# Batch 1's transposes, first projections and values placed between the first row maxima of an attention and mixture-of-experts kernel

## What is computed

```python
x = L0_attn_x                                   # (4, 512, 256)
mod = (_silu(L0_c) @ L0_wmod).reshape(L0_c.shape[0], 6, 1, -1)
sa, ca, ga, sb, cb, gb = (mod[:, 0], mod[:, 1], mod[:, 2], mod[:, 3], mod[:, 4], mod[:, 5])
ga = (2 * (ga >= 0) - 1) * jnp.maximum(jnp.abs(ga), 0.25)      # gb in the same way
h = _layernorm(x, axis=-1) * (1 + ca) + sa
x = x + ga * _L0_attn_ref(h, wq, wk, wv, wo)    # 16 heads of 16, scores without a scale, softmax
h = _layernorm(x, axis=-1) * (1 + cb) + sb
x = x + gb * _L0_ffn_ref(h, ...)                # shared expert and the top 4 of 32 experts
```

## Time and profile before

| | us |
|---|---|
| median of 3 runs (604.32 to 607.96) | 604.84 |
| the profiled execution, as a run | 604.01 |
| its span, first to last instruction | 602.2 |
| TensorE busy | 563.6 (94%) |
| VectorE busy | 370.8 (62%) |
| ScalarE busy | 255.3 (42%) |
| mean granted TensorE clock | 0.974 |

### The profile page before, as it was taken

The page is one execution under the profiler, slowest core; times in us unless marked ns, Lnnn a source line. Parts: engine busy times, 40 slices in busy tenths (PEclk is TensorE's granted clock), DMA queues, the critical chain, the costliest instruction groups (busy, mean ns, idle before and its releaser), DMA issues.

```text
span 602.2 us, 10736 instructions
## 1 busy us (share of the span) xinstructions
PE 563.6 (94%) x3118; PEld 313.8 (52%) x3119; DVE 370.8 (62%) x860; ACT 255.3 (42%) x519; POOL 217.8 (36%) x284
## 2 busy tenths in 40 slices
PE   4889999999999999999999999998999999999881
PEld 3443233333333333333343465668888898897570
DVE  6385677778589785898855569435444444443683
ACT  3113545564765647555568140022343443433000
POOL 6100000000110751108434653441675666667332
PEclk9966999999999999999999999999999999999996
DMA  7242126100501224012101169524555645540791
GB/s 227 42 132 97 34 54 188 37 11 10 115 4 34 93 70 115 7 31 90 53 1 41 66 267 330 147 82 130 158 157 151 182 144 165 166 124 9 269 371 58
DMA packets 42343, 67.18 MB, mean 112 GB/s; under 512 B 9291, under 2 KB 32212, under 8 KB 41948
## 3 DMA queue, kind: packets, MB, share of 16 engines
q1 hardware_dynamic: 30208, 45.62, 25.9%
q0 software_dynamic: 7680, 16.87, 8.2%
q10 hardware_dynamic: 4416, 4.20, 2.1%
HBM read 38.93 MB, written 27.51 MB: 110 GB/s over the span
## 4 chain that ended last, share of the span: by engine, by line
PE 81%; DVE 8%; issue 3%; DMA 3%; SPq 1%; ACT 1%; POOL 1%; ACTq 0%; POOLq 0%; DVEq 0%
PE ps L863 23%; PE ps L876 10%; PE ps L1089 9%; PE ps L1110 6%; PE ps L960 6%; PE ps L812 5%; PE ps L954 3%; PE ps L834 3%; PE ps L1075 3%; PE ps L821 3%; PE ps L889 3%; DVE max_q L1201 2%; PE ps L1100 2%; PE ps L798 2%; PE ps L919 1%
## 5 line engine op out<-in xcount | busy, mean ns | idle before, releaser
L1201 DVE TENSOR_REDUCE max_q<-ps 128x1 f32<-128x512 f32 x256 | 163.8, 686 | 74.5 <-PE ps L834 72.8
L691 ACT ACTIVATE probs<-ps 128x512 f32<-128x512 f32 x256 | 138.0, 596 | 99.5 <-PE ps L863 99.2
L834 PE MATMUL ps<-k_rows,q_rows 31*128 31x512 f32 x512 | 149.7, 678 | 1.8 <-DMA k_rows<-qk_raw 1.8
L863 PE MATMUL ps<-q_rows,k_rows 32*128 32x512 f32 x512 | 147.6, 646 | 0.9 <-DVE max_q L1201 0.9
L545 POOL DMA_INDIRECT results<-y_sb,dest x96 | 94.5, 984 | 64.8 <-issue 35.0
L863 PEld LDWEIGHTS ps<-q_rows,k_rows 32*128 32x128 f32 x512 | 42.9, 186 | 71.6 <-ACT probs L691 52.2
L1089 PE MATMUL ps<-up_sb,oT 128*128 x384 | 70.7, 328 | 1.5 <-DVE oT L1565 1.3
L876 PE MATMUL ps<-probs,v_ext 128*32 128x512 f32 x512 | 68.2, 605 | 1.1 <-ACT probs L691 1.1
L1089 PEld LDWEIGHTS ps<-up_sb,oT 128*128 128x128 f32 x384 | 61.4, 191 | 2.1 <-issue 1.9
L1110 PE MATMUL ps<-down_sb,e_hidT 96*128 x192 | 49.8, 383 | 3.8 <-ACT e_hidT L748 3.8
L498 POOL TENSOR_TENSOR rstd<-veps,mhalf 128x4 f32<-128x4 f32 x4 | 4.1, 1036 | 134.3 <-DVE veps L1283 132.4
(11 more groups left out here) (180 smaller groups left out, 695.7 us busy)
## 6 DMA issues: line engine op xcount, KB each, us to landing
xe<-dispatched SPq DMA_DIRECT2D x96, 129.0 KB, 2.1
up_sb<-results SPq DMA_DIRECT2D x16, 512.0 KB, 7.9
up_sb<-in_up SPq DMA_DIRECT2D x2, 3072.0 KB, 15.1
dispatched<-pad_rows SPq DMA_DIRECT2D x33, 129.0 KB, 4.5
down_sb<-in_down SPq DMA_DIRECT2D x1, 3072.0 KB, 31.3
x<-in_x ACTq DMA_DIRECT2D x4, 512.0 KB, 5.1
q_rows<-qk_raw SPq DMA_DIRECT2D x64, 32.0 KB, 1.9
k_rows<-qk_raw SPq DMA_DIRECT2D x64, 32.0 KB, 1.9
```

The costliest lines, as they stand in the source:

```text
L691: act.activation(probs[:, u % 8, :], ps[:, st_bank(t.b, g, u), :], ACT.Exp).then_inc(exp_done, 1)
L834: pe.matmul(ps[:, banks[u % len(banks)], :], q_rows[32 * i:32 * i + ONE, b % 2, g, qt * P:(qt + 1) * P], k_rows[32 * i:32 * i + ONE, b % 2 ...
L863: pe.matmul(ps[:, st_bank(b, g, n), :], k_rows[32 * i:32 * i + 32, b % 2, g, kt * P:(kt + 1) * P], q_rows[32 * i:32 * i + 32, b % 2, g, :] ...
L1201: dve.tensor_reduce(max_q[:, g % 2, qt, i:i + 1], ps[:, banks[(16 * g + n) % len(banks)], :], AXX, ALU.max).then_inc(max_done, 1)
```

## The change

In the lead, batch 1's TP0, TP1, QK0, QK1 and V0 are computed between the 16 scores of group 0 and behind them. Only six scores of group 1 are made before turn 0 (22 in all, `AHEAD_BY`), and the turn begins when 16 maxima are done. Places 0 to 4 (`CATCH`) of turn 0 then issue four scores each, 22 to 41; from place 5 on it is two, the same ones as before. `FIRST` no longer has TP0, TP1, QK0, QK1 and V0; MAX0 goes from place 0 to 5, V1 from (27, 29) to 7, QK2 from (19, 21) to 13, QK3 from 23 to 19; V1 and QK2 are no longer split. ACT's work follows: it normalises batch 1 before the lead's values, and the new work goes ahead of and behind the negation of the first maxima. VectorE finishes batch 1's statistics ahead of its first maximum. On SP the first maxima go ahead of the fourth group's rows, batch 1's q rows ahead of MAX0, its k rows ahead of MAX1, and the shared expert's weights behind the two broadcasts. `raw_qk` waits for the rows of two groups instead of four. `scoreT` number 2 waits for batch 1's V0, the new last use of bank 7.

```diff
@@ -55,10 +55,12 @@
-    LEAD = ("TP0", "TP1", "QK0", "QK1", "QK2", "QK3", "V0", "V1", "MAX3")
-
-    FIRST = {"MAX0": 0, "TP0": 1, "TP1": 3, "QK0": 5, "QK1": 7, "MAX1": 8, "MOD0": 9, "MOD1": 11, "V0": (13, 15),
-             "MAX2": 16, "MODT": 17, "QK2": (19, 21), "QK3": 23, "MAX3": 24, "V1": (27, 29), "NT0": 30, "NT1": 31}
+    LEAD = ("TP0", "TP1", "QK0", "QK1", "QK2", "QK3", "V0", "V1")
+
+    AHEAD = {"TP0": 0, "TP1": 1, "QK0": 0, "LEAD_MAX": 1, "QK1": 0, "V0": 1}
+
+    FIRST = {"MAX0": 5, "V1": 7, "MAX1": 8, "MOD0": 9, "MOD1": 11, "QK2": 13, "MAX2": 16, "MODT": 17, "QK3": 19,
+             "MAX3": 24, "NT0": 30, "NT1": 31}
@@ -80,6 +82,9 @@
         elif self.att:
+            if self.mod:
+                for name, m in self.AHEAD.items():
+                    self.take(name, m, used)
             half = 0
@@ -286,12 +291,15 @@
         fin = Finish(B, used)
+        lead.uses["MAX3"] = turns[0].uses.pop("LEAD_MAX")
         turn_of = dict(zip(range(-1, B + 1), [lead, *turns, fin]))
...
         ONE = P // G - 1
+        AHEAD_BY = 22
+        CATCH = 5
@@ -323,6 +331,17 @@
             return h2T[:, s, k, :] if s < B - 1 else h2T_late[:, k, :]
+
+        def scores_at(t, place):
+
+
+            if t.mod and place < CATCH:
+                ahead = range(AHEAD_BY + 4 * place, AHEAD_BY + 4 * place + 4)
+            elif place < 16 or t.pre:
+                ahead = (32 + 2 * place, 33 + 2 * place)
+            else:
+                ahead = ()
+            return [(t.b + u // 64, u // 16 % NG, u % 16) for u in ahead]
@@ -380,16 +399,21 @@
+                if t.mod:
+                    for g in range(2):
+                        place_rows(t, 0, g)
                 max_rows(t, 0)
-                if t.pre:
+                if t.mod:
+                    for g in range(2):
+                        place_rows(t, 1, g)
+                elif t.pre:
                     place_rows(t, 0, 0)
                     place_rows(t, 0, 1)
-                if t.mod:
-                    place_rows(t, 1, 0)
-                    place_rows(t, 1, 1)
                 max_rows(t, 1)
...
                     modulation_out()
+                    for w_d, w_s in ((sgate, sgate_sb), (sup, sup_sb), (sdown, sdown_sb)):
+                        sp.dma_start(w_s[:, :, :], w_d.rearrange("(k p) n -> p k n", p=P)).then_inc(sh_ld, 16)
                 elif t.pre:
@@ -407,14 +431,13 @@
             for g in range(NG):
+                if g == NG - 1:
+                    max_rows(lead, 3)
                 for c in range(2):
...
                 sp.dma_start(w_s[:, :, :], w_d.rearrange("(k p) n -> p k n", p=P)).then_inc(w_ld, 16)
-            max_rows(lead, 3)
-            for w_d, w_s in ((sgate, sgate_sb), (sup, sup_sb), (sdown, sdown_sb)):
-                sp.dma_start(w_s[:, :, :], w_d.rearrange("(k p) n -> p k n", p=P)).then_inc(sh_ld, 16)
             for t in turns:
@@ -581,9 +604,9 @@
                 src = full(act, t, f"QK{c}")
-                if c == 0:
-
-                    for g in range(NG):
+                if c % 2 == 0:
+
+                    for g in (c, c + 1):
                         above(act, rows_ld[g], 128 * (t.b + 1))
@@ -656,8 +679,9 @@
-                if t.att and place % 8 == 0 and (place < 24 or t.pre):
-                    negate_max(t, place // 8)
+                for g in range(NG):
+                    if t.at(f"MAX{g}", place):
+                        negate_max(t, g)
                 for k in range(KD):
@@ -713,11 +737,16 @@
                 raw_qk(lead, c)
+            act.wait_ge(nmr_s, 2)
+            normalise(turns[0])
             for m in range(2):
                 values_out(lead, m)
+            for k in range(KD):
+                to_hT(turns[0], f"TP{k}", 1)
+            raw_qk(turns[0], 0)
             negate_max(lead, 3)
-            act.wait_ge(nmr_s, 2)
-            normalise(turns[0])
+            raw_qk(turns[0], 1)
+            values_out(turns[0], 0)
             for t in turns:
@@ -858,7 +887,7 @@
-                        written(pe, lead, "V1")
+                        written(pe, turns[0], "V0")
                     above(pe, exp_done, 64 * b + u - 2)
@@ -968,8 +997,9 @@
                         values(t.b if g else t.b - 1, (g - 1) % NG, TJ - 1)
-                if place % 8 == 0 and (g < 3 or t.pre):
-                    turn_max(t, g)
+                for group in range(NG):
+                    if t.at(f"MAX{group}", place):
+                        turn_max(t, group)
                 for k in range(KD):
@@ -1006,11 +1036,8 @@
                         if step == 2:
-                            for n in (u, u + 1):
-                                if g < 2:
-                                    score(t.b, g + 2, n)
-                                else:
-                                    score(t.b + 1, g - 2, n)
+                            for b, group, n in scores_at(t, 8 * g + u // 2):
+                                score(b, group, n)
                         for n in range(u, u + step, 2):
@@ -1041,13 +1068,20 @@
                 score(0, 0, n, SC + ST[0:2])
-                if n in (3, 7):
+                if n in (3, 6):
                     project_v(lead, n // 4)
+                if n in (8, 9):
+                    tokens_to_columns(turns[0], f"TP{n - 8}", 1)
+                if n == 12:
+                    project_qk(turns[0], 0)
             turn_max(lead, 3)
-            for n in range(16):
-                score(0, 1, n, SC + ST[0:2])
-
-            pe.wait_ge(max_done, 32)
+            project_qk(turns[0], 1)
+            for n in range(AHEAD_BY - 16):
+                score(0, 1, n)
+                if n == 1:
+                    project_v(turns[0], 0)
+
+            pe.wait_ge(max_done, 16)
             pe.wait_ge(ones_ld, 16)
@@ -1500,14 +1534,10 @@
             def turn(t):
-                for g in range(NG):
-                    for u in range(16):
-                        if g < 2:
-                            score_max(t.b, g + 2, u)
-                        elif t.pre:
-                            score_max(t.b + 1, g - 2, u)
-                        if u % 2:
-                            between(t, 8 * g + u // 2)
+                for place in range(32):
+                    for b, group, n in scores_at(t, place):
+                        score_max(b, group, n)
+                    between(t, place)
@@ -1548,11 +1578,11 @@
             st.did(dve.tensor_copy(tails[:, :, :, 0], home[:, :].rearrange("p (t k) -> p t k", k=TOPK)))
+            minus_mean_over_deviation(TJ, NT, 2)
             for n in range(16):
                 score_max(0, 0, n, SC + ST[0:2])
-            minus_mean_over_deviation(TJ, NT, 2)
-            for n in range(16):
-                score_max(0, 1, n, SC + ST[0:2])
+            for n in range(AHEAD_BY - 16):
+                score_max(0, 1, n)
             for t in turns:
...
             finish(fin)
```

## The result

| | before | changed |
|---|---|---|
| median, us | 604.57 (13 runs) | 608.70 (13 runs, 605.95 to 620.04) |
| ratio | | 1.0069, 95% interval 1.0044 to 1.0093 |
| profiled execution: as a run, span, mean granted clock | 604.01, 602.2, 0.974 | 611.80, 610.0, 0.984 |

The change makes the kernel slower, by 0.7%; I had forecast 602.2 with a range of 599.5 to 606.5. The changed kernel was run again beside the last experiments (label changed_again): 607.59, ratio 1.0070 (1.0042 to 1.0097). The profile of that set has the clock at full from the lead on and is the cleaner one to read: 605.46 as a run, span 603.7. I call it *the changed kernel at full clock*, and the first one *the first profile*. In two of the later sets (halves to grouped32_halves; grouped22_halves and split_v_again) every kernel, the one before too, took 8% longer, so of these only ratios and the starts of places are used.

The account below looks back on a forecast made before the run. TensorE, busy 94%, was taken to bound the kernel, held up by VectorE's row maxima from 30.9 to 49.0 us. Gains of 1.85 and 0.76 made 2.6 us: 604.84 - 2.6 = 602.2, range 599.5 to 606.5.

Parts of the forecast that it names:

- part 2: From 24.75 us to place 5: turn 0 starts 4.75 us earlier, catch-up returns 2.9, place 5 at 59.5; gain 1.85 us.
- the walk: Part 2's step-by-step timing of lead and catch-up at full clock: 16th maximum at 38.4, turn 0 at 44.3, place 5 at 59.5.
- Part 1: Places 5 to 31: 6.16 us of TensorE work gone, six newly empty places cost 0.90 us each; net gain 0.76 us.
- six microseconds for real: First rival: newly empty places of turn 0 do not wait, gain 1.85 + 6.16 = 8.0 us, 596.8; chance 0.14.
- outer bound of the walk: Latest begin of place 5: 0.65 us for each maximum and bubbles of 2 us give 60.6, gain 0.75 us.
- inner bound: Earliest begin of place 5: 22 maxima at 0.603 after 44.3 without bubbles, then the values, give 58.6, gain 2.75 us.
- second rival: Clock falls in TensorE's wait at 36 us, QK1 takes 3.76 us instead of 1.92: +1.8, 604.0; chance 0.17.
- third rival: Clock falls in places 0 to 4 and stays low, the three-bank loop costs 5.8 us more: 608.0; chance 0.11.
- Part 3: What could be late next: (a), (b) and (c), checked from place 5 on; nothing taken off the gain.
- (a): MAX0 at place 5 must reach q_rows by place 8: landed 65.5, place 8 at 66.7; costs nothing, by 1.2 us.
- (b): Shared weights behind mod_b's broadcast, needed at place 18: slack 1.5 us, fair share costs at most 2.5; nothing taken.
- (c): VectorE in places 20 to 29: 20 maxima and extras take 16.5 us against five pairs of 4.03; covered.

Follow-up runs that it names:

- halves: Changed kernel with V1, QK2 and QK3 split into halves at places (5, 7), (13, 15), (19, 21) and MAX0 at place 4; ratio 1.0039.
- grouped32_halves: Changed kernel without catch-up: all 32 first scores in the lead in fours, moved work between them, V1, QK2, QK3 halved; ratio 0.9934, repeated 0.9960.
- grouped22_halves: grouped32_halves with the catch-up put back: 22 scores in the lead, V0 whole behind the last, four scores in places 0 to 4; ratio 1.0004.
- split_v_again: split_v run once more in a later set, four runs; ratio 0.9866.
- split_v: grouped32_halves with batch 1's V0 in two halves, behind scores 24 and 28 instead of both behind 24; 597.92 us, ratio 0.9896.
- all32: Changed kernel with all 32 first scores made before turn 0 through five banks and no catch-up; 614.48 us, ratio 1.0176.
- weights_early: Changed kernel with the shared expert's weights loaded before turn 0, as in the kernel before; four runs, 605.79 to 620.16 us, no ratio.
- qk1_first: Changed kernel with batch 1's QK1 ahead of the transpose of the first maxima instead of behind it; 606.39 us, ratio 1.0033.
- qk1_halves: Changed kernel with both QK1 ahead of the first transpose of maxima and V1, QK2, QK3 in halves; ratio 0.9950.
- six_only: Kernel before with only 22 scores ahead and four in places 0 to 4, batch 1's work left in turn 0; 621.01 us, ratio 1.0291.

## Why the prediction was wrong

The step that failed is part 2: the start of turn 0 came 2.7 us later than the walk had it, and the catch-up behind it took 2.0 us longer. The clock, which the sum took at full, fell in most runs on top of that (mean clock 0.989 or less in ten of thirteen, against 0.993 in the profile without a fall in turn 0).

**What bounds the kernel.** The reading of the rows held: VectorE's maxima bound 31 to 49 us, TensorE the turn.

**Part 1, places 5 to 31.** Right, and the tenth by some luck: 0.76 us forecast, 64.5 to 63.7 (0.8) measured at full clock. Two small terms cancelled. V1, whole, was counted as 2.12 us; the pair of place 7 took 5.27 us with it and 5.26 with QK1 (1.92) before. And place 15, empty now, gave nothing back (4.94 us for its pair in both), where 0.16 was due. The rival *six microseconds for real* is refuted: the pairs of places 5, 21 and 27 took 4.03 or 4.04 us, that of 23 took 4.24 with the transpose of MAX3 in it and that of 29 took 4.62 with NT0. The chain of the first profile in places 22 to 24, of which 23 is newly empty:

```profile
111.02 1.36 PE ps L892 x3
112.99 1.00 PE ps L905 x8
115.06 1.36 PE ps L892 x3
117.03 1.00 PE ps L905 x8
```

from 111.02 to 115.06 are two places, 4.04 us as in the earlier trace rows. halves then took three of the waits away again.

**Part 2, the start of turn 0.** Forecast 44.3, measured 47.0 at full clock. Three terms of the walk were mis-sized. First, I let a score cost 0.27 us in any company, from four in 1.14. The rows show 1.05 to 1.06 us for one, two or three scores ahead of a full-width matmul. The lead of the changed kernel breaks 16 scores into six groups, which cost 6.5 us where I took 4.3; the 16th maximum comes at 40.06, not 38.4 (1.7 us). Second, the two scores behind QK1 cost 1.06 instead of 0.53. Third, I gave the six scores of group 1 the lead's five banks; the diff shows `score(0, 1, n)` without them, three banks, so that the last of the six waits for a maximum (46.19 to 46.87 in the chain): about 0.8 us. The three add up to 3.0, and 0.3 come back: from the 16th maximum to the end of QK1 I had 2.3 us (38.4 to 40.7), and the chain has 2.04 (40.06 to 42.10). That makes the 2.7.

**Part 2, the catch-up.** Forecast 15.2 us from the turn's begin to place 5, measured 17.2. Score 22 went out 0.9 us behind the turn's begin, where I had 1.25. From it to score 41 the timeline has 47.96 to 62.15 = 14.2 us, where I had 12.65: 18 steps took 0.67 us each and not 0.61 (1.1 us), and the one bubble, behind the `values` of place 2, was 0.4 us longer than my 0.75 and 0.3 together. Behind score 41, I let 0.27 us for it and the `values` follow; it cost 1.05 us ahead of them, 0.8 us more, by the same wrong term as in the lead. The mechanism was right, a loop through three banks with 0.2 us of slack; I sized it as if it kept its best pace through every place boundary. grouped22_halves against split_v puts its cost at 3 us. The outer bound of the walk, 60.6 for place 5, was also added up wrong: it leaves out the 1.0 us of `values` that the inner bound has, and with it is 61.6, slower than before. The QK0 of the walk ends at 35.2 by its own terms, not 35.4. With both parts the forecast of place 5 was 59.5 and the profile has 64.3; from 1.85 us of gain it became 2.9 of loss, which part 1 brings to 2.1 at turn 1 and 1.5 in the span.

**The clock.** The sum took it at full. The second rival, the fall in the wait at 36 us, came about in four of the five profiles with that wait (the first one, all32, weights_early, halves; not changed_again), though I gave it 0.17, and cost 3.3 us, not 1.8: V0 and two scores were low too. That the wait brings this fall about is borne out by qk1_first and qk1_halves, which have no such wait and begin turn 0 at 45.3 and 45.6. The fall in the places themselves, the third rival, did not come in the changed kernel at places 0 to 4; it came in six_only, and for 3 us at place 18 in the first profile and in qk1_first. There MODT's narrow matmuls stand near newly empty places; halves, which fills them, did not show it, but neither did changed_again, weights_early and all32, so its cause is only argued. The runs of the changed kernel at a mean clock of 0.991 to 0.993 take 605.5 to 607.5 us, those at 0.984 or 0.985 take 610.8 to 611.8. So of the 4.1 us between the medians the profile at full clock shows 1.5 as the kernel's own, from the catch-up and the lead; most of the rest I put to the falls of the clock. The two profiles of the same kernel bear that out in part: their spans lie 6.3 us apart, and 4.6 of these have come by turn 1, 3.0 with the fall at 40 us and 1.6 with the one at place 18. The 1.7 us behind turn 1 stay open: the granted clock is 1.00 there in both up to 500 us. No run took the falls away alone (qk1_first, which keeps the clock at 40 us, also starts the turn earlier).

The Trainium skill (TensorE: Matmul & The Clock Gate, "A second HAM failure mode: psum-queue depth-cycling") tells of a kernel whose clock swings between its two levels while it cycles through PSUM banks. The changed kernel's loop at full clock does not show it: the granted clock was 1.00 through all 17 us of its three banks. In six_only the clock was at half through most of that loop's 31 us, but it had fallen before the loop began, between 36 and 38 us. So no run here shows such a loop bringing the clock down.

**Part 3.** (a) held: place 8 waited for nothing in the first profile, although MAX0's rows were issued at 69.60, 2.4 us behind the begin of place 5. (b) held: mod_b landed 11.0 us behind its issue, and nothing waited at place 18. (c) held: places 20 to 29 took no longer than the pairs of 4.0 us and their extras.

**The way the loss went.** Taken by itself the idea of moving the work is sound: split_v moves the same transposes, projections and values, and gains 6 us. By the starts in its profile 1.7 us come from the start of turn 0, 2.2 from places 0 to 4, where the kernel before still ran at half clock up to about 55 us, and 3.1 from places 5 to 31, where halves fill three of the six empty places. What failed in the change is the sum that balanced an earlier start against maxima still owed.

## What to carry to other kernels

Where one engine's queue of small results (here 42 row maxima) must be done before a point, starting the next stage earlier with some of them owed is only worth it if the stage can take them at the same pace; count the banks there, and size the loop from a row in which it runs, not from its best case. When filler is put among narrow matmuls that run side by side on strips of the array, put it between full groups: here a lone one cost as much as four. And where a schedule waits for a round trip between two engines (here the exp that frees a bank), an emptied slot does not give back all of its work: price it from a slot that is empty already.

## What the runs showed of the hardware

- One, two or three scores of 31 rows ahead of a full-width matmul took 1.05 to 1.06 us, four took 1.07 to 1.15 (changed_again, split_v).
- The granted clock differs between executions of one kernel: places 0 to 4 of grouped32_halves took 11.3 us in one and 15.6 in another, its runs 597.8 to 605.2 at a mean clock of 0.992 to 0.977. A wait of TensorE of some 2 us at 38 us was followed by a fall in most profiles and not in all.
- In the loop through three banks one maximum took 1.4 us at half clock (six_only) against 0.70 at full clock. Letting only the matmul double had given 0.92.
